# A four-layer graph network on one core: group-wise hand-over of sums, drains on VectorE, in-degree and self loops in other stages

## The reference, cut to what matters

```python
# layer 0: attention over incoming edges, two weights blended by an edge attribute
m = h_fwd[src] * attr[:, 0:1] + h_rev[src] * attr[:, 1:2]           # 64 columns
p = exp(leaky_relu(m @ attn.T) - max)                               # 4 heads
out[h] = segment_sum(m * p[:, h] / segment_sum(p)[dst], dst)
# layer 1: neighbours' mean of rows cut to their 32 largest entries
out = x @ W_self + segment_sum(maxk(x @ W_neigh)[src], dst) / max(deg, 1)
# layer 2: 16 relations, forward by dst and backward by src, each a mean; self loop twice
out = 2 * x @ loop + bias + mean_dst((x @ Wf[type])[src]) + mean_src((x @ Wb[type])[dst])
# layer 3: two graph-transformer layers of 8 heads by src, between two projections
```

## Time and profile before

| | us |
|---|---|
| median of the timed runs | 7,348.49 |
| their range | 7,345.13 to 7,369.44 |
| span of the profiled execution | 8,945.4 |
| busy there: POOL | 5,223.0 (58%) |
| PE, and its weight loads | 5,070.2 (57%), 3,398.4 (38%) |
| DVE | 4,560.5 (51%) |
| ACT | 1,221.8 (14%) |

### The profile page before, as it was taken

How to read it: one execution, slowest core, us unless ns; L and a number is a source line. 1 busy time by engine, 2 the same in 40 slices (tenths; PEclk the granted TensorE clock), 3 DMA queues, 4 the chain that set the end, 5 groups by cost and what they waited for, 6 DMA issues and landing times.

```text
span 8945.4 us, 80437 instructions
## 1 busy us (share of the span) xinstructions
PE 5070.2 (57%) x17709; PEld 3398.4 (38%) x17709; DVE 4560.5 (51%) x11322; ACT 1221.8 (14%) x4092; POOL 5223.0 (58%) x5325
## 2 busy tenths in 40 slices
PE   4444444455554159677776655556555556555555
PEld 2333332222232024344444433325555545554554
DVE  5665567666663014444444333335555555555555
ACT  3555552000000000000000000002111112111112
POOL 4666661566666730666666666664666654666664
PEclk7776777677766579788888766667777777677777
DMA  3222221333322025444444333332222223222222
GB/s 83 47 48 47 46 47 30 87 91 90 89 80 62 19 70 166 136 133 134 132 133 112 90 90 90 91 90 75 81 83 83 83 80 76 81 81 82 81 81 68
DMA packets 499429, 753.18 MB, mean 84 GB/s; under 512 B 217891, under 2 KB 351257, under 8 KB 498713
## 3 DMA queue, kind: packets, MB, share of 16 engines
q0 software_dynamic: 236352, 604.00, 24.3%
q1 hardware_dynamic: 262616, 144.15, 5.6%
HBM read 622.95 MB, written 124.79 MB: 84 GB/s over the span
## 4 chain that ended last, share of the span: by engine, by line
PE 30%; another core or an unknown queue 23%; issue 20%; DVE 12%; SPq 8%; POOL 3%; DMA 2%; DVEq 2%; ACT 1%; POOLq 0%; ACTq 0%
PE ps L301 17%; SPq L1429 7%; DVE acc L289 5%; PE ps L2019 4%; PE ps L926 3%; POOL rows L249 3%; PE ps L1319 2%; PE ps L1310 2%; DVE onehot L270 1%; DMA rows<-table2b,slots_s 1%; DVEq L275 1%; DVEq L289 1%; DVE top L519 1%; SPq L1425 1%
## 5 line engine op out<-in xcount | busy, mean ns | idle before, releaser
L289 DVE TENSOR_TENSOR acc<-acc,ps 128x257 f32 (+3 forms) x4992 | 1880.3, 377 | 2656.2 <-remote 1460.7
L301 PE MATMUL ps<-rows,onehot 128*128 128x257 f32 (+1 forms) x4992 | 1845.6, 504 | 1435.6 <-issue 714.6
L249 POOL DMA_INDIRECT rows<-table,slots_d x1664 | 1631.7, 981 | 1050.6 <-issue 485.2
L301 PEld LDWEIGHTS ps<-rows,onehot 128*128 128x128 f32 x4992 | 1069.0, 239 | 2272.3 <-issue 1312.9
L301 PE MATMUL ps<-msg,onehot 128*128 128x136 f32 (+1 forms) x4992 | 1258.1, 414 | 740.1 <-remote 374.1
L301 PEld LDWEIGHTS ps<-msg,onehot 128*128 128x128 f32 x4992 | 1003.8, 259 | 973.5 <-issue 816.1
L249 POOL DMA_INDIRECT rows<-table2f,slots_d x832 | 804.0, 966 | 764.7 <-DMA table2f<-big 326.5
L249 POOL DMA_INDIRECT rows<-table3b,slots_s x832 | 828.0, 995 | 538.6 <-DVE msg L1372 283.2
L249 POOL DMA_INDIRECT rows<-table3a,slots_s x832 | 828.5, 996 | 526.3 <-DVE msg L1372 274.3
L249 POOL DMA_INDIRECT rows<-table2b,slots_s x832 | 798.2, 959 | 437.6 <-issue 225.0
L1319 PE MATMUL ps<-big,msg 128*128 x3328 | 635.4, 351 | 631.3 <-issue 433.6
(11 more groups left out here) (310 smaller groups left out, 4185.7 us busy)
## 6 DMA issues: line engine op xcount, KB each, us to landing
table2f<-big SPq DMA_DIRECT2D x80, 640.0 KB
table2b<-msg SPq DMA_DIRECT2D x200, 256.0 KB
rows<-table,slots_d POOLq DMA_INDIRECT x1664
slots_d<-recs_d SPq DMA_DIRECT2D x832, 2.5 KB
rows<-table2f,slots_d POOLq DMA_INDIRECT x832
rows<-table2b,slots_s POOLq DMA_INDIRECT x832
rows<-table3a,slots_s POOLq DMA_INDIRECT x832
rows<-table3b,slots_s POOLq DMA_INDIRECT x832
```

Of the source, the lines that this page charges most:

```text
L249: nc.gpsimd.indirect_dma_start(out=rows[:, j, 0:width], out_offset=None, in_=table[:, :], in_offset=bass.IndirectOffsetOnAxis(ap=slots[:, ...
L289: nc.vector.tensor_tensor(acc[:, bass.ds(b * width, width)], acc[:, bass.ds(b * width, width)], ps[:, bank + k, 0:width], ALU.add).then_in ...
L301: nc.tensor.matmul(ps[:, bank + k, 0:width], onehot[:, h, k, :], rhs, start=True, stop=True).then_inc(sem(of(s, "tile_sum")), 1)
```

## The change

- The hand-over is by group: PE increments `group_sum` after the fourth product, DVE `group_added` after the fourth add. PSUM holds two groups in every stage: in e1, e2f and attention two tiles share a bank (256 columns each), in e0 and e2b the sums take all eight banks.
- DVE's waits for itself become drains: one before every add, one before each of the operations in e0, attention and the sort that read what DVE has just written.
- In e1, e2f and e2b the one-hot matrices are made two groups ahead, and the adds of group n follow in one piece.
- The column of ones moves to e0 (261 columns instead of 260); e1 sums 256 columns instead of 257.
- The self-loop products move to e2f, one block after the second of its eight pairs, in bank 7; the backward products then have three banks. e2b's one-hot reads `iota` in SBUF.

```diff
-        def adder(dve, s, block, n, bank, width, whole=False):
+        def sum_of(s, n, k, width):
+            if s in ("e0", AGAIN, "e2b"):
+                return ps[:, G * (n % 2) + k, 0:width]
+            first_bank = 4 if s in ATTENTIONS else 0
+            at = k % 2 * 256
+            return ps[:, first_bank + n % 2 * 2 + k // 2, at:at + width]
+
+        def adder(dve, s, block, n, width):
             of_tile = tile_blocks(block, n, mybir.EngineType.DVE)
             def add(k):
                 b = of_tile[k]
-                if not whole or k == 0:
-                    after(dve, of(s, "tile_sum"), tiles0[s] + n * G + (G if whole else k + 1))
-                after(dve, of(s, "tile_added"), tiles0[s] + n * G + k)
-                nc.vector.tensor_tensor(acc[:, bass.ds(b * width, width)], acc[:, bass.ds(b * width, width)],
-                                        ps[:, bank + k, 0:width], ALU.add).then_inc(sem(of(s, "tile_added")), 1)
+                if k == 0:
+                    after(dve, of(s, "group_sum"), groups0[s] + n + 1)
+                dve.drain()
+                added = nc.vector.tensor_tensor(acc[:, bass.ds(b * width, width)], acc[:, bass.ds(b * width, width)],
+                                                sum_of(s, n, k, width), ALU.add)
+                if k == G - 1:
+                    added.then_inc(sem(of(s, "group_added")), 1)
...
+        def sum_group(pe, s, n, h, width, rhs):
+            after(pe, of(s, "group_added"), groups0[s] + max(n - 1, 0))
+            for k in range(G):
+                last = nc.tensor.matmul(sum_of(s, n, k, width), onehot[:, h, k, :], rhs(k), start=True, stop=True)
+            last.then_inc(sem(of(s, "group_sum")), 1)
...
         def sum_dve(dve, s, slots, words, block, width, loop=groups):
+            for n in range(AHEAD):
+                next_one_hot(dve, s, slots, words, n)
             def body(n, h):
-                later = not isinstance(n, int) or n > 0
-                if later:
-                    add = adder(dve, s, block, n - 1, 0, width)
-                    add(0)
-                after(dve, "tile_sum", tiles0[s] + G * (n - R + 1))
-                one_hot(dve, s, slots, words, n, h)
-                if later:
-                    for k in range(1, G):
-                        add(k)
+                next_one_hot(dve, s, slots, words, n + AHEAD)
+                add_group(dve, s, block, n, width)
...
-        def top_of(dve, r, steps):
-            after(dve, "gs_replaced", steps + 1)
-            dve.nop(nofuse=True)
-            nc.vector.max(top8[:, r, :], left).then_inc(sem("gs_top"), 1)
+        def top_of(dve, r):
+            dve.drain()
+            nc.vector.max(top8[:, r, :], left)
...
                 nc.vector.tensor_tensor(qk3[:, h, :, :], ps[:, 2 + h % 2, :].rearrange("p (g d) -> p g d", d=D),
-                                        rows4[:, h, :, 0:D], ALU.mult).then_inc(sem("att_qk"), 1)
+                                        rows4[:, h, :, 0:D], ALU.mult)
                 add(0)
-                dve.wait_ge(sem("att_qk"), start + n + 1)
+                dve.drain()
                 nc.vector.tensor_reduce(att[:, 0, :], qk3[:, h, :, :].rearrange("p g (a d) -> p (g a) d", d=HD),
-                                        AX.X, ALU.add).then_inc(sem("att_red"), 1)
+                                        AX.X, ALU.add)
                 add(1)
-                dve.wait_ge(sem("att_red"), start + n + 1)
+                dve.drain()
...
+                    if q == SELF_AT:
+                        self_pe(pe, m)
                 sum_pe(pe, "e2f", C, lambda eng, body: groups_beside(eng, body, pb))
                 pe.wait_ge(sem("e2f_done"), 1)
-                pe.wait_ge(sem("loop_twice"), 1)
-                sum_pe(pe, "e2b", C + 1, lambda eng, body: groups_then(eng, body, self_pe))
+                sum_pe(pe, "e2b", C + 1)
```

More of the change, by code:

```diff
@@ L137, in gnn_program @@
         here_sum = ps[:, 4, 0:P]
-        here = {"e1": here_sum, "e2f": iota[:, :], "e2b": here_sum, "e3a": iota[:, :], "e3b": iota[:, :]}
+        here = {"e1": here_sum, "e2f": iota[:, :], "e2b": iota[:, :], "e3a": iota[:, :], "e3b": iota[:, :]}
         x3 = x_sb[:, :].rearrange("p (b c) -> p b c", c=C)
@@ L295, in add_tiles, with add_group @@
+                dve.drain()
[3 more added lines that the diff above has]
+                    added.then_inc(sem(of(s, "group_added")), 1)
+            return add
+        def add_group(dve, s, block, n, width):
+            add = adder(dve, s, block, n, width)
             for k in range(G):
                 add(k)
[L298 to L302, removed]
+        def sum_group(pe, s, n, h, width, rhs):
[3 more added lines that the diff above has]
+            last.then_inc(sem(of(s, "group_sum")), 1)
@@ L305, in sum_pe @@
         def sum_pe(pe, s, width, loop=groups):
             def body(n, h):
-                after(pe, "tile_onehot", groups0[s] + n + 1)
+                after(pe, "tile_onehot", onehots0[s] + n + 1)
                 after(pe, f"rows_ready{h}", gathered(s, n, h))
-                for k in range(G):
-                    sum_tile(pe, s, n, h, k, 0, G, width, rows[:, h * G + k, 0:width])
+                sum_group(pe, s, n, h, width, lambda k: rows[:, h * G + k, 0:width])
             loop(pe, body)
+        AHEAD = 2
@@ L666, in gnn_program @@
         W0 = HEADS * F0 + HEADS
+        W0D = W0 + 1
         def e0_act(act, s):
@@ L699, in body @@
             def body(n, h):
[L700 removed]
                 after(pe, of(s, "e0_weighted"), n + 1)
                 after(pe, of(s, "e0_weighted_act"), n + 1)
[L703 to L704 removed]
+                sum_group(pe, s, n, h, W0D, lambda k: msgA[:, h, k, 0:W0D])
             return body
@@ L1314, in queries @@
                 after(pe, "att_oneT", start + n + 1)
-                after(pe, "att_qk", start + n - 1)
+                after(pe, "att_att", start + n - 1)
                 of_tile = tile_blocks(block_s, n, mybir.EngineType.PE)
@@ L1324, in sums @@
                 after(pe, "att_res", start + n + 1)
-                for k in range(G):
-                    sum_tile(pe, s, n, h, k, 4, G, W3, res3[:, h, k, :])
+                sum_group(pe, s, n, h, W3, lambda k: res3[:, h, k, :])
             def step(n, h, left):
@@ L1630, in _ @@
                 groups_beside(act, lambda n, h: None, pb_xt)
-                act.wait_ge(sem("loop_loaded"), 16 * 3)
-                nc.scalar.activation(w_loop, w_loop, ACT.Copy, scale=2.0).then_inc(sem("loop_twice"), 1)
-                for m in range(NB):
-                    self_act(act, m)
             if layers > 3:
@@ L1785, in group @@
                 def group(n, h, begin=plain, end=plain):
-                    later = not isinstance(n, int) or n > 0
-                    if later:
-                        add = adder(dve, "e1", block_d, n - 1, 0, C + 1)
-                        add(0)
-                    after(dve, "tile_sum", tiles0["e1"] + G * (n - R + 1))
-                    one_hot(dve, "e1", slots_d, KD, n, h)
+                    next_one_hot(dve, "e1", slots_d, KD, n + AHEAD)
+                    add = adder(dve, "e1", block_d, n, C)
                     begin(n)
-                    if later:
-                        for k in range(1, G - 1):
-                            add(k)
+                    for k in range(G - 1):
+                        add(k)
                     end(n)
-                    if later:
-                        add(G - 1)
+                    add(G - 1)
+                for n in range(AHEAD):
+                    next_one_hot(dve, "e1", slots_d, KD, n)
                 for n in range(R):
```

148 lines of the change are left out of this document (66 added, 82 removed).

## The result

The changed kernel takes 7,472.98 us (7,467.43 to 7,474.70, four runs) where the kernel before takes 7,348.05 (7,345.13 to 7,369.44): 1.0164 times as long, interval 1.0152 to 1.0176, or 125 us more. The forecast was 7,367 in a range of 7,290 to 7,560, slower with a chance of 0.45. So the time lies in the range, but it came by a rival's way, not by the forecast's.

What follows compares the result with a forecast made beforehand. The prediction took POOL's gather pace to bound the timed kernel almost throughout. Stage ends (4 us) and e2b's one-hot (15 us) gave +19, so 7,348 + 19 = 7,367 us, in a range of 7,290 to 7,560.

Steps and rivals of the forecast that it cites:

- The base: Six gather stages: the timed kernel runs at POOL's gather pace almost throughout; 4,992 gathers need 6,413 us.
- the 1,259 us of waits: Gather windows of the profiled execution: time beyond POOL's 6,413 us, taken as absent from timed runs.
- The drains: e0, attention, sort groups: DVE's cycle grows to 5.2, 5.07 and 4.9 us, hidden behind POOL; cost 0.
- The hand-over by group: All gather stages: one hand-over a group gains 0 and costs 4 us, at the ends of e1, e2f and e2b.
- rival A: e0, attention, sort groups: drains tip DVE over POOL's pace, +163 us, 7,511 us; chance 0.36.
- e2b's one-hot: e2b: reading iota from SBUF lengthens POOL's gathers by 18 ns each, 15 us, bounds 0 and 20.
- stage ends: Ends of e1, e2f, e2b: DVE starts adding the last group only after four products, 3 x 1.4 = 4 us.
- Self loops: e2f: the moved matmuls bring PE to 4.6 to 4.8 us a group, under POOL's 5.09; cost 0.
- B: Hand-over: timed runs do wait there, so the change is faster, 7,298 us or 7,230; chance 0.16.
- C: e2f: PE becomes the bound at half clock, 60 us, 7,430 us; chance 0.05.

Runs made afterwards that it cites:

- e0: Not a run: one of the kernel's six stages that gather rows, 208 groups of four gathers; its window takes 1,076 us in the changed kernel.
- cut kernel before: Kernel before with one gather a group instead of four from the fifth group of each stage on: 5,321.38 us.
- cut changed kernel: Changed kernel with one gather a group instead of four from the fifth group of each stage on: 6,634.95 us.
- drains alone: Kernel before with DVE's self-waits made drains, hand-over tile by tile: 6,882.27 us with one gather a group, 9,064.61 us (1.0130) whole.
- the edit alone: Kernel before with only e2b's one-hot reading the numbers from SBUF instead of PSUM: 8,922.69 us, ratio 0.9981.
- hand-over by group alone: Changed kernel with semaphores again in place of attention's six drains, hand-over by group kept: 9,029.65 us, 1.0093 of before.

## Why the prediction was right or wrong

**The base: right in its sum, wrong in its reason.** POOL's pace over six stages was put at 6,413 us. The cut kernel before spends 931.6 us outside its gather windows (5,319.5 less 4,387.9); taken from the 7,346.3 us of the kernel before in the same set this leaves 6,415. But the prediction took the 1,259 us of waits for a mark of the profiled execution, absent from timed runs. At the slow level the timed runs have it too, and at the quick level the profiled run, 7,474.70 us, is among the timed ones. What makes the slow level stays open; the record has a span and a granted clock for every timed run, so recording isn't excluded as a part of it. The traces give one hint: for the same changed kernel the one at the quick level holds 113,928 semaphore updates and 103,706 of DMA queues, that at the slow level 33,662 and 26,629, so the slow one's records are incomplete; and with about a quarter of the gathers the late semaphores in attention were all but gone. The Trainium skill, "NOTIFIC — the notification-queue block", section "Overflow: three behaviours, one of which stalls the engine", knows a mode in which a record queue that is full holds the engine back. No run here shows that it was this. By the same section that mode drops no record, while the slow trace holds fewer. Against it also stands that the cut kernel's scatters, with few gathers around them, still took 736 us with the projection, where the quick level has 415.

**The drains: right in what they cost, in attention by two misses that cancel.** A gap of 0.21 before adds was taken, 0.17 to 0.18 is measured; for fixed addresses 0.10 was taken, and behind an add the reduction starts 0.07 us after it. e0's cycle was put at 5.16, and 5.2 with the fourth group's extra drain; it is 5.06 in most groups, and 5.17 in the mean of the cut changed kernel:

```profile
504.55 0.44 DVE L739 TENSOR_TENSOR big<-big 128x272 f32<-128x272 f32 x1
...
509.61 0.44 DVE L739 TENSOR_TENSOR big<-big 128x272 f32<-128x272 f32 x1
```

Attention's was put at 5.07 and is 5.05 with drains alone, 4.98 in the changed kernel. That is luck in part: the base of 3.55 is 3.30 in the cut kernel before (its reductions start at 4205.74, 4209.05 and 4212.35 us), and the drains add 1.75 and not 1.52, with a seventh gap, of 0.18 before L1341, that the forecast hadn't counted. e1's mean was put at 4.9 and is 4.6. In the changed kernel none passes POOL's pace, as said. The Trainium skill, "VectorE: DVE Perf Modes", section "Rules for kernel authors", says to minimise operations and not semaphores. The prediction read it as making drains free too, though the page gives no price for an explicit drain. They are not free: attention without POOL goes from 3.36 to 5.08 us a group by the drains, with the same operations.

**The hand-over by group: here the forecast failed**, in the sentence "In e0 and the attention stages a weighting comes between, 0". That sentence counted the wait once, at a stage's end. But the weighting stands inside every group, and behind it the first add waits for four products, each group. The loop was in rival A, sized at 20 us, with 62 more for attention from a drain's gap of 0.26. Its size is 1,125.8 + 1,123.8 less twice POOL's 1,082 of the forecast: 86 us (over the 1,073 that after's own gathers need it is 104; the kernel before has no windows at the quick level that would say which). The 20 came from reckoning PE at its full clock and a little over. The granted clock of these stages is 0.81 and 0.82: part of the time PE is at the lower of its two levels, 1.2 instead of 2.4 GHz (0.50 in the window at 5602 us), where four products take 2.18 us and the loop 5.89. In the cut kernel before, whose PE is busy 586 of 698 us there, the clock is 0.99.

**e2b's one-hot**: 15 us forecast, bounds 0 and 20; 823.4 less 798.2 is 25 us, outside the bounds. e2f's value was taken for it because both read SBUF, but in one and the same run, that of the edit alone, e2f is at 957 ns and e2b at 986. Why e2b is hit harder is not shown; that its one-hot falls beside more gathers would be one reason.

**The rest**: stage ends 4 us, measured 8 (7,472.9 less windows of 6,533 is 940, against 931.6). e0 at 1,076 instead of 1,082, e1 1,061 instead of 1,057. Self loops: without POOL e2f goes from 3.5 to 3.8 us a group, far under 5.09; cost 0, as said, though PE's pace had been put at 4.6 to 4.8. e2f is at 1,070 instead of 1,059: its gathers need 1,045, and one wait of POOL of 26 us at its start, for the preparation of the sources' places, is in the cut kernel before as well, with 22.

**The sum**: attention 86, e2b 25, the stage ends and what lies between 8, the other windows about 9 by the forecast's own values: 128, against 125 measured. The forecast had 19. **Rivals**: A came true in attention alone, and by its smaller term; its main one, a gap of 0.24 us or more, did not occur. Its sign was half right: POOL waited for DVE in attention, but DVE did idle, for PE. B, that the kernel before waits at the hand-over in timed runs, is refuted for the quick level by 6,415 against 6,413, and POOL's gap is 0.30 us there too. C did not occur: e2f had a granted clock of 0.97.

That it takes both edits to pass POOL's pace rests on four corners: neither edit 3.36 us a group, drains alone 5.08, hand-over by group alone 4.5, both 5.39. The first and the last are of the quick level, the other two of the slow one; the third is from the table above, whose four corners, all at the slow level, say the same (3.9, 5.1, 4.5, 5.7). What stays argued is that mending attention would give its 86 us back at the quick level.

## What to carry to other kernels

An engine that isn't the bound has room that can be measured: take most of the bound engine's work away and read the pace that is left (here 3.36 against 5.16 us). Two edits may each fit into that room and not fit together, so add their costs in one cycle before calling either free. And when a consumer waits for a batch instead of its first item, look for the loop in which the batch's producer waits for the consumer's previous step: the longer wait is paid in every turn, and at the clock that the producer then has.

## What the hardware showed unexpectedly

- The same program takes 7,348 us in one set of runs and 8,908 to 8,974 in others, with the same durations of single gathers (0.95 us) and adds (0.42); the difference is idle time, much of it where semaphores come late, and a stretch of scatters of 681 instead of 415 us. Both levels were seen under one chip number.
- A drain between two adds leaves 0.17 us idle, less than the 0.21 that a semaphore of DVE to itself left there; but a semaphore whose writer lies one operation back lets the next operation start 0.08 us before the end of the one in front, and behind a drain no add of the trace of after starts less than 0.16 us after it.
- POOL's gathers of 0.95 us are stretched, some to 1.5 us, where DVE compares from SBUF with SBUF; with the numbers in PSUM they hardly are (957 against 986 ns in one set of runs). The Trainium skill, "GPSIMD Engine Reference", section "Key points", says that the two engines share their ways into SBUF and meet there when DVE has two inputs in SBUF; the two means agree with it.
